# The last batch's order of work is rearranged on three engines, and its tile counts and a weight split move behind it

## The chip, the cores and the metric

The kernel runs on one core of a Trainium2 chip. The metric is the device time of one execution in microseconds, lower is better.

## The reference

Input `x` is 8 batches of 512 tokens, 256 wide. With `xn = layernorm(x)` the output is

```
out = x + attention(xn) + experts(xn)

attention: q, k, v of 16 heads, 16 wide; features elu(q.proj)+1, elu(k.proj)+1 (128 per head)
           kv = sum over tokens of k' v;  attn = q' kv / (q' . sum k');  attn @ W_out.T + b_out
experts:   logits = xn @ Wr + br; the two best of 8 experts, softmax weights over them
           h = gelu(xn @ W1[e] + b1[e]);  sum over e of weight * (h @ W2[e] + b2[e])
```

## The kernel before, in words

Every engine has its own program, and semaphores join them. Matmuls on fp32 data are done as three products of a high and a low part (`mm3`, lines 527 to 529). Banks of PSUM are `F[0..3]`, `WK[0..1]`, `NUM` and `DEN`.

**Attention, batch by batch.** A batch `b` has 32 units `u`. `unit` makes one matmul group into `F[u % 4]`: the k features of a token block for `u < 16` (from the stacked tensor `Sk`), a head's q features for `u >= 16` (from `Sq`). ScalarE's `exp(b, u)` (line 1063) and VectorE's `features(b, u)` (line 1468) turn it into `kp` or `qp`; unit `u` waits until feature `u - 4` is done. Into these 32 units the remaining steps are placed by hand, each engine with its own table of "if u == ...". A batch's attention is finished inside the next batch's units: `attend` (line 623, four groups of heads), ScalarE's `copy_att`, `to_tokens` (632), VectorE's `reciprocals` and `products` (1474, 1480), `to_heads` (640), `at_hi`, `heads_rest` (647), `at_lo`, `project` (24 products), `residual` (1489). The own batch's state is made by four `kv` blocks (605), `copy_kv`, `state_T` (613) and `state`.

`final_iteration(7)` does this for the last batch. TensorE has room there, and `keep_clock` (line 772) puts matmuls without use into it. VectorE also makes the routing tables there: `row_counts`, `blocks_1` to `blocks_5`, `first_tiles_of(1..8)`, `short_blocks` and `tile_table`, a chain of small instructions in which `join()` waits for the one before. `tile_table` raises `route_rdy`.

**Experts.** Tokens were sent to the rows of their experts in DRAM (`xg`) by GpSimd. Then 25 tiles of up to 384 rows run: `ffn1` (eight chunks), gelu, high and low part of h (`hh`, `hl`, line 1740), `ffn2` (three blocks of rows), and GpSimd adds the rows into the output. Tile 0 of expert 0 is mixed with the end of the last batch's attention in a written order on TensorE: `ffn1_last(0)`, `attend(7, 3)`, `ffn1_last(1..3)`, `to_tokens`, `ffn1_last(4..6)`, `to_heads`, `ffn1_last(7)`, `heads_rest`, `ffn2(0,0,0)` for chunks 0 to 5, `project`, and then `ffn2(0,0,0)` for chunks 6 and 7. The last of these needs `hidden_lo(0, 3)`, which stands behind `turn_rows(1)` on VectorE:

```
        hidden_lo(0, 1)
        hidden_lo(0, 2)
        turn_rows(1)
        hidden_lo(0, 3)
```

`turn_rows(1)` (line 1507) waits until tile 1's rows (`gblk`, `gtok`) are loaded.

**Weights and rows.** Expert 0's weights are loaded in two halves, the first when unit 15 is done (semaphore `f_full`), since it takes the memory of `Sk`. GpSimd splits them into high and low parts in four pieces (`split_weights`, lines 1905 and 1907); the second raises `w1_rdy`, the fourth `w_rdy`. SP's queue then runs in this order:

```
        sp.wait_ge(w_rdy, 1)
        load_raw(1)
        sp.wait_ge(route_rdy, 1)
        for e in range(E - 1):
            pad(e + 1)
            other_rows(e)
```

`load_raw(1)` asks for expert 1's 2 MB, `pad` writes zero rows, and `other_rows(0)` loads tile 1's rows once VectorE has freed the last ones (`grow_free`).

Of the kernel before, what the change touches and what calls it, by code (L numbers as in the profile page):

```python
# [25 lines left out]
P = 128  # L26
# [47 lines left out]
def build(nc, x, w_in, proj, w_out, b_out, experts, b1, b2, br, consts, out):  # L74
# [144 lines left out]
    ATT_LAST = [NUM, DEN, WK[0], WK[1]]  # L219
# [304 lines left out]
    def _(pe):  # L524
# [102 lines left out]
        def to_tokens(b, n):  # L627

            if n == 0:
                pe.wait_ge(att_rdy, 4 * b + 4)  # L630
            for c in range(4):
                last = nc.tensor.transpose(TOK_BANK[n][:, c * P:(c + 1) * P], att_sb[:, c, n * P:(n + 1) * P], ident)
            last.then_inc(tok_full, 1)
# [16 lines left out]
        def project(b, i, banks=PROJ_BANK):  # L650

            if i == 0:
                pe.wait_ge(atl_rdy, 2 * b + 2)
            for n in range(2):
# [4 lines left out]
            last.then_inc(proj_full, 1)  # L659
# [115 lines left out]
        def final_iteration(b):  # L775
            for u in range(32):
                unit(b, u)
                if 15 <= u < 22:
                    keep_clock(WK[0])
                if 23 <= u < 28:  # L780
                    keep_clock(DEN)
                if u == 29:
                    pe.wait_ge(att_rdy, 4 * b + 1)
                if u >= 29:
                    keep_clock(NUM)
                if u == 0:
                    pe.wait_ge(o_rdy, 2 * b - 1)
                    attend(b - 1, 2)
                if u == 1:
                    pe.wait_ge(pos_read, b + 1)  # L790
                    attend(b - 1, 3)
                if u == 2:
# [4 lines left out]
                if u == 5:  # L797
                    to_tokens(b - 1, 0)
                    to_tokens(b - 1, 1)
                    to_tokens(b - 1, 2)  # L800
                if u == 7:
                    pe.wait_ge(pos_read, b + 2)
                    to_tokens(b - 1, 3)
                if u == 8:
                    pe.wait_ge(at_rdy, 4 * b - 2)
                    kv(b, 0)
                if u == 10:
                    to_heads(b - 1, 0)
                    to_heads(b - 1, 1)
                if u == 11:  # L810
                    kv(b, 1)
                if u == 12:
                    heads_rest(b - 1, 0)
                    heads_rest(b - 1, 1)
                if u == 14:
                    project(b - 1, 0)
                    project(b - 1, 1)
                if u == 15:
                    kv(b, 2)
                if u == 19:  # L820
                    kv(b, 3)
                if u == 22:
                    pe.wait_ge(kv_rdy, b + 1)
                    state_T(b)
                if u == 24:
                    pe.wait_ge(state_rdy, b + 1)
                    pe.wait_ge(o_rdy, 2 * b + 2)
                    attend(b, 0, ATT_LAST)
                if u == 27:
                    first_rows_T()  # L830
                if u == 28:
                    attend(b, 1, ATT_LAST)
                if u == 31:
                    pe.wait_ge(gxl_rdy, 1)
# [136 lines left out]
        pe.wait_ge(w1_rdy, 1)  # L971
        ffn1_last(0)
# [41 lines left out]
    def _(act):  # L1014
# [136 lines left out]
        def final_iteration(b):  # L1151
            for u in range(32):
                exp(b, u)
                if u == 0:
                    copy_att(b - 1, 1)
                    copy_att(b - 1, 2)
                if u == 1:
                    copy_att(b - 1, 3)
                if u == 9:
                    at_hi(b - 1, 0)  # L1160
                    at_hi(b - 1, 1)
                if u == 11:
                    at_lo(b - 1, 0)
                    at_lo(b - 1, 1)
                if u == 19:
                    copy_kv(b)
                if u == 22:
                    state(b)
                if u == 24:
                    copy_att(b, 0, ATT_LAST)  # L1170
                if u == 28:
                    first_rows_hi()
# [123 lines left out]
    def _(dve):  # L1296
# [173 lines left out]
        def reciprocals(b, n):  # L1470

            dve.wait_ge(tok_full, NT * b + n + 1)
            heads = TOK_BANK[n][:, :].rearrange("p (h c) -> p h c", c=32)
            V.reciprocal(rec[:, n, :], heads[:, :, HD]).then_inc(rec_rdy, 1)

        def products(b, n):

            dve.wait_ge(rec_rdy, NT * b + n + 1)
            heads = TOK_BANK[n][:, :].rearrange("p (h c) -> p h c", c=32)
# [104 lines left out]
        def final_iteration(b):  # L1584
            dve.sem_inc(hl_rdy, 4)
            dve.sem_inc(y_rdy, SUB)
            for u in range(32):
# [3 lines left out]
                if u == 3:  # L1591
                    reciprocals(b - 1, 0)
# [392 lines left out]
```

## Time and profile before

| | us |
|---|---|
| median of 3 runs (lowest to highest) | 700.12 (699.78 to 701.21) |
| the profiled execution's own time | 700.86 |
| its span, first to last instruction | 698.7 |
| TensorE (PE) busy | 682.9 |
| VectorE (DVE) busy | 504.1 |
| ScalarE (ACT) busy | 475.3 |
| GpSimd (POOL) busy | 227.9 |

Times of rows count from the span's start. The last batch runs from about 265 to 298 us, tile 0 from there to 323 us, and the other 24 tiles to the end. The span is 2.16 us shorter than that execution's own time. A matmul's busy time overlaps that of the next; the distance between two starts tells the rate.

### The profile page before, as it was taken

How to read it: one execution, taken by the hardware profiler on the slowest of the kernel's cores; microseconds unless marked ns; L12 is line 12 of the kernel's file. 1: busy time of each engine (PE TensorE's matmuls, PEld its weight loads, DVE VectorE, ACT ScalarE, POOL GpSimd, SP SyncE). 2: the span in 40 equal slices, each digit the busy share in tenths (PEclk: the TensorE clock that was granted, in tenths of full speed). 3: DMA queues.
4: the chain of work that ended last, by engine and by line, in shares of the span. 5: the costliest groups of instructions: out<-in, count | busy, mean ns of one | idle time of the engine just before them, and what ended most of it. 6: DMA issues, size and time to landing. Idle time of an engine off the chain costs nothing.

```text
span 698.7 us, 17362 instructions
## 1 busy us (share of the span) xinstructions
PE 682.9 (98%) x5503; PEld 603.3 (86%) x5504; DVE 504.1 (72%) x1246; ACT 475.3 (68%) x875; POOL 227.9 (33%) x169
## 2 busy tenths in 40 slices
PE   8899999999999998999999999999999999999996
PEld 4666777777777776589999999999999999999996
DVE  8798888888888878748577675556777545577544
ACT  5687969696969696776557775447775444577553
POOL 2053232323232324643232532225233222322422
PEclk9999999999999999999999999999999999999999
DMA  8856474747474647765455663336556333454531
GB/s 266 200 182 170 108 228 106 228 106 228 106 228 106 198 106 223 224 189 142 100 98 118 145 167 46 46 47 106 178 71 167 48 52 53 81 131 107 69 48 23
DMA packets 87205, 91.65 MB, mean 131 GB/s; under 512 B 60049, under 2 KB 73361, under 8 KB 84897
## 3 DMA queue, kind: packets, MB, share of 16 engines
q1 hardware_dynamic: 71426, 59.36, 33.9%
q0 software_dynamic: 13872, 18.75, 15.2%
q10 hardware_dynamic: 1872, 13.11, 5.1%
q8 instruction: 17, 0.28, 0.2%
q14 instruction: 18, 0.15, 0.1%
HBM read 39.32 MB, written 26.67 MB: 94 GB/s over the span
## 4 chain that ended last, share of the span: by engine, by line
PE 82%; DVE 6%; issue 4%; ACT 2%; POOL 2%; DMA 2%; SPq 1%; POOLq 0%; DVEq 0%
PE F L527 9%; PE F L528 9%; PE F L529 9%; PE WK L527 5%; PE F L596 5%; PE WK L529 4%; PE WK L528 4%; PE NUM L527 4%; PE NUM L529 4%; PE NUM L528 4%; PE DEN L605 4%; PE DEN L527 4%; PE DEN L529 4%; PE DEN L528 4%; PE F L590 3%
## 5 line engine op out<-in xcount | busy, mean ns | idle before, releaser
L1932 POOL DMA_INDIRECT out<-ysb,icur x75 | 121.0, 1613 | 270.6 <-DVE ysb L1763 241.0
L1218 ACT ACTIVATE h<-F,b1c 128x384 f32<-128x384 f32 x200 | 112.2, 575 | 140.0 <-PE F L529 131.2
L1740 DVE TENSOR_TENSOR hl<-h,hh 128x768 fp32r<-128x768 f32 x100 | 96.1, 962 | 111.6 <-ACT hh L1222 111.6
L1063 ACT ACTIVATE e_ring<-F 128x512 f32<-128x512 f32 x256 | 145.7, 621 | 38.5 <-PE F L590 35.0
L527 PE MATMUL F<-gxh,wh 128*128 128x384 f32 (+1 forms) x400 | 128.6, 321 | 0.4 <-DVE wl L1641 0.4
L528 PE MATMUL F<-gxl,wh 128*128 128x384 f32 (+1 forms) x400 | 128.0, 320 | 0.0
L529 PE MATMUL F<-gxh,wl 128*128 128x384 f32 (+1 forms) x400 | 128.0, 320 | 0.0
L1866 POOL DMA_INDIRECT xg<-rows,slots x64 | 63.2, 988 | 174.0 <-PE F L590 158.8
L1468 DVE SCALAR_TENSOR_TENSOR kp<-F,e_ring 128x512 f32<-128x512 f32 x128 | 82.7, 680 | 13.2 <-PE DEN L605 6.2
L1468 DVE SCALAR_TENSOR_TENSOR qp<-F,e_ring 128x512 f32<-128x512 f32 x128 | 85.2, 683 | 8.5 <-ACT e_ring L1063 7.0
L1222 ACT ACTIVATE hh<-h 128x768 fp32r<-128x768 f32 x100 | 84.6, 846 | 3.3
L527 PEld LDWEIGHTS F<-gxh,wh 128*128 128x128 f32 x400 | 75.6, 189 | 2.5 <-issue 2.5
L528 PEld LDWEIGHTS F<-gxl,wh 128*128 128x128 f32 x400 | 75.6, 189 | 0.0
L529 PEld LDWEIGHTS F<-gxh,wl 128*128 128x128 f32 x400 | 75.6, 189 | 0.0
L590 PEld LDWEIGHTS F<-stacked_proj,Sk 97*128 97x128 f32 x256 | 38.0, 192 | 26.0 <-issue 13.9
L527 PE MATMUL DEN<-wh,hh 128*128 128x256 f32 x200 | 56.7, 283 | 0.6 <-issue 0.6
L527 PE MATMUL NUM<-wh,hh 128*128 128x256 f32 x200 | 56.6, 283 | 0.2 <-DVE hl L1740 0.2
L528 PE MATMUL DEN<-wl,hh 128*128 128x256 f32 x200 | 56.6, 283 | 0.0
L529 PE MATMUL DEN<-wh,hl 128*128 128x256 f32 x200 | 56.6, 283 | 0.0
L529 PE MATMUL NUM<-wh,hl 128*128 128x256 f32 x200 | 56.5, 283 | 0.0
L528 PE MATMUL NUM<-wl,hh 128*128 128x256 f32 x200 | 56.5, 282 | 0.0
L596 PE MATMUL F<-Sq,stacked_proj 97*128 97x512 f32 x128 | 52.3, 450 | 0.3 <-DVE qp L1468 0.3
(261 smaller groups left out, 1552.6 us busy)
## 6 DMA issues: line engine op xcount, KB each, us to landing
wraw<-experts ACTq DMA_DIRECT2D x12, 1024.0 KB, 6.2
gblk<-xg SPq DMA_DIRECT2D x100, 96.0 KB
Sk<-kdh SPq DMA_DIRECT2D x64, 128.0 KB, 2.3
Sq<-qdh SPq DMA_DIRECT2D x64, 128.0 KB
xin<-x SPq DMA_DIRECT2D x8, 512.0 KB, 5.5
Sk<-kdl SPq DMA_DIRECT2D x32, 128.0 KB, 2.4
Sq<-qdl SPq DMA_DIRECT2D x32, 128.0 KB
xres<-x SPq DMA_DIRECT2D x8, 512.0 KB
```

Of the source, the lines that this page charges most:

```text
L527: nc.tensor.matmul(dst, wh_, mh_, start=first, stop=False)
L528: nc.tensor.matmul(dst, wh_, ml_, start=False, stop=False)
L529: return nc.tensor.matmul(dst, wl_, mh_, start=False, stop=last)
L590: last = nc.tensor.matmul(F[u % 4][:, s * D:(s + 1) * D], Sk[0:SROWS, place_of(pr), n * P:(n + 1) * P], stacked_proj[0:SROWS, 2 * pr:2 * p ...
L596: last = nc.tensor.matmul(F[h % 4][:, :], stacked_proj[0:SROWS, h, :], Sq[0:SROWS, place_of(h // 2), :], start=True, stop=True)
L1063: A(e_ring[:, u % 4, :], F[u % 4][:, :], ACT.Exp, bias=EXP_BIAS, scale=1.0 / DOWN).then_inc(exp_done, 1)
L1218: A(h32[:, m, :], F[m % 4][:, 0:T], ACT.Gelu, bias=b1c[:, w, m:m + 1]).then_inc(gelu, 1)
L1222: A(hh[:, 2 * q:2 * q + 2, :], h32[:, 2 * q:2 * q + 2, :], ACT.Copy).then_inc(hh_rdy, 1)
L1468: V.scalar_tensor_tensor(dst, F[u % 4][:, :], DOWN, e_ring[:, u % 4, :], ALU.max, ALU.min).then_inc(feat, 1)
L1740: V.tensor_tensor(hl[:, 2 * q:2 * q + 2, :], h32[:, 2 * q:2 * q + 2, :], f32(hh[:, 2 * q:2 * q + 2, :]), ALU.subtract).then_inc(hl_rdy, 1)
L1866: pool.indirect_dma_start(xg, bass.IndirectOffsetOnAxis(slots[:, k:k + 1], 0), rows[:, n, :], None, bounds_check=last_row, oob_is_err=Fals ...
L1932: pool.indirect_dma_start(out, bass.IndirectOffsetOnAxis(icur[:, s, :], 0), ysb[:, s, :], None, bounds_check=last_token, compute_op=ALU.ad ...
```

## The change

On all three engines `final_iteration` gets another table. On TensorE `attend(6, 2)` and `attend(6, 3)` stand behind units 2 and 3 (before: 0 and 1), the tokens of batch 6 behind unit 6, its heads behind unit 12. `project(6)` moves from behind unit 14 into four pieces behind units 19 to 22; `state_T` from unit 22 to 20, and the last batch's first attention group from 24 to 22. `keep_clock` goes from fifteen places to six. The tokens' and attention's banks change (`TOK_LAST`, `ATT_LAST`). The wait for `gxl_rdy` moves from `attend(7, 2)` to `ffn1_last(0)`.

On VectorE the routing steps from `blocks_3` on move behind the last feature, as `tile_counts()`; the eight single additions of `first_tiles_of` become three over eight columns. `first_rows_tokens` moves ahead of them, and `hidden_lo(0, 0)` behind the last batch's products. On GpSimd the third split gets a wait for `route_rdy`.

The diff, with unchanged lines cut, and without the two places that give `to_tokens`, `reciprocals` and `products` a parameter for their banks:

```diff
@@ -216,7 +216,8 @@
     PROJ_BANK = [WK[1], NUM]
-    ATT_LAST = [NUM, DEN, WK[0], WK[1]]
+    ATT_LAST = [DEN, NUM, DEN, WK[1]]
+    TOK_LAST = [WK[1], NUM, WK[0], WK[1]]
     PROJ_LAST = [WK[1], WK[0]]
...
@@ -647,16 +648,17 @@
-        def project(b, i, banks=PROJ_BANK):
-
-            if i == 0:
+        def project(b, i, banks=PROJ_BANK, blocks=range(2)):
+
+            if i == 0 and blocks[0] == 0:
                 pe.wait_ge(atl_rdy, 2 * b + 2)
-            for n in range(2):
+            for n in blocks:
                 tok = slice((2 * i + n) * P, (2 * i + n + 1) * P)
...
                                WOh[:, g, :], WOl[:, g, :], g == 0, g == 1)
-            last.then_inc(proj_full, 1)
+            if blocks[-1] == 1:
+                last.then_inc(proj_full, 1)
...
@@ -775,63 +777,67 @@
                 unit(b, u)
-                if 15 <= u < 22:
-                    keep_clock(WK[0])
-                if 23 <= u < 28:
-                    keep_clock(DEN)
-                if u == 29:
-                    pe.wait_ge(att_rdy, 4 * b + 1)
-                if u >= 29:
-                    keep_clock(NUM)
-                if u == 0:
+                if u == 2:
                     pe.wait_ge(o_rdy, 2 * b - 1)
                     attend(b - 1, 2)
-                if u == 1:
-                    pe.wait_ge(pos_read, b + 1)
-                    attend(b - 1, 3)
-                if u == 2:
+                if u == 3:
                     pe.wait_ge(o_rdy, 2 * b)
...
                                      start=True, stop=True).then_inc(pos_full, 1)
-                if u == 5:
-                    to_tokens(b - 1, 0)
-                    to_tokens(b - 1, 1)
-                    to_tokens(b - 1, 2)
+                    pe.wait_ge(pos_read, b + 1)
+                    attend(b - 1, 3)
+                if u == 6:
+                    to_tokens(b - 1, 0, TOK_LAST)
+                    pe.wait_ge(pos_read, b + 2)
+                    to_tokens(b - 1, 1, TOK_LAST)
+                    to_tokens(b - 1, 2, TOK_LAST)
                 if u == 7:
-                    pe.wait_ge(pos_read, b + 2)
-                    to_tokens(b - 1, 3)
+                    kv(b, 0)
                 if u == 8:
-                    pe.wait_ge(at_rdy, 4 * b - 2)
-                    kv(b, 0)
+                    pe.wait_ge(at_rdy, 4 * b - 3)
+                    to_tokens(b - 1, 3, TOK_LAST)
                 if u == 10:
+                    pe.wait_ge(feat, 32 * b + 8)
+                    kv(b, 1)
+                if u == 12:
                     to_heads(b - 1, 0)
                     to_heads(b - 1, 1)
-                if u == 11:
-                    kv(b, 1)
-                if u == 12:
+                if u == 15:
+                    kv(b, 2)
                     heads_rest(b - 1, 0)
                     heads_rest(b - 1, 1)
-                if u == 14:
-                    project(b - 1, 0)
-                    project(b - 1, 1)
-                if u == 15:
-                    kv(b, 2)
+                if u == 16:
+                    keep_clock(NUM)
+                if u in (24, 25):
+                    keep_clock(WK[0])
+                if u == 18:
+                    pe.wait_ge(feat, 32 * b + 16)
+                    kv(b, 3)
                 if u == 19:
-                    kv(b, 3)
-                if u == 22:
+                    project(b - 1, 0, blocks=(0,))
+                if u == 20:
+                    project(b - 1, 0, blocks=(1,))
                     pe.wait_ge(kv_rdy, b + 1)
                     state_T(b)
-                if u == 24:
+                if u == 21:
+                    project(b - 1, 1, blocks=(0,))
+                if u == 22:
+                    project(b - 1, 1, blocks=(1,))
                     pe.wait_ge(state_rdy, b + 1)
+                    pe.wait_ge(feat, 32 * b + 20)
+                    attend(b, 0, ATT_LAST)
+                if u == 26:
+                    pe.wait_ge(o_rdy, 2 * b + 1)
+                    first_rows_T()
+                if u == 27:
                     pe.wait_ge(o_rdy, 2 * b + 2)
-                    attend(b, 0, ATT_LAST)
-                if u == 27:
-                    first_rows_T()
-                if u == 28:
                     attend(b, 1, ATT_LAST)
+                if u == 29:
+                    pe.wait_ge(att_rdy, 4 * b + 1)
+                if u >= 29:
+                    keep_clock(DEN)
                 if u == 31:
-                    pe.wait_ge(gxl_rdy, 1)
                     attend(b, 2, ATT_LAST)
...
@@ -969,6 +975,7 @@
         pe.wait_ge(w1_rdy, 1)
+        pe.wait_ge(gxl_rdy, 1)
         ffn1_last(0)
...
@@ -1153,23 +1160,25 @@
                     copy_att(b - 1, 1)
+                if u == 2:
                     copy_att(b - 1, 2)
-                if u == 1:
+                if u == 3:
                     copy_att(b - 1, 3)
-                if u == 9:
+                if u == 13:
                     at_hi(b - 1, 0)
                     at_hi(b - 1, 1)
-                if u == 11:
+                if u == 16:
                     at_lo(b - 1, 0)
                     at_lo(b - 1, 1)
-                if u == 19:
+                if u == 18:
                     copy_kv(b)
-                if u == 22:
+                if u == 20:
                     state(b)
-                if u == 24:
+                if u == 23:
                     copy_att(b, 0, ATT_LAST)
+                if u == 27:
+                    first_rows_hi()
                 if u == 28:
-                    first_rows_hi()
                     copy_att(b, 1, ATT_LAST)
...
@@ -1588,49 +1597,45 @@
                     dve.sem_inc(grow_free, 1)
-                if u == 3:
-                    reciprocals(b - 1, 0)
-                    reciprocals(b - 1, 1)
-                    products(b - 1, 0)
+                if u == 4:
                     row_counts()
-                if u == 4:
-                    products(b - 1, 1)
-                    reciprocals(b - 1, 2)
+                if u == 6:
+                    reciprocals(b - 1, 0, TOK_LAST)
+                    reciprocals(b - 1, 1, TOK_LAST)
+                    products(b - 1, 0, TOK_LAST)
+                if u == 7:
+                    products(b - 1, 1, TOK_LAST)
+                    reciprocals(b - 1, 2, TOK_LAST)
+                if u == 8:
+                    products(b - 1, 2, TOK_LAST)
+                if u == 9:
+                    reciprocals(b - 1, 3, TOK_LAST)
+                if u == 10:
+                    products(b - 1, 3, TOK_LAST)
+                if u == 12:
                     blocks_1()
-                if u == 5:
-                    products(b - 1, 2)
-                    blocks_2()
-                if u == 6:
-                    reciprocals(b - 1, 3)
-                    blocks_3()
-                    products(b - 1, 3)
-                if u == 8:
-                    blocks_4()
-                if u == 8:
-                    blocks_5()
-                if u == 9:
-                    first_tiles_of(1)
-                    first_tiles_of(2)
-                if u == 10:
-                    first_tiles_of(3)
-                    first_tiles_of(4)
-                    first_tiles_of(5)
-                if u == 11:
-                    first_tiles_of(6)
-                    first_tiles_of(7)
-                    first_tiles_of(8)
-                    short_blocks()
-                if u == 17:
-                    tile_table()
+                if u == 13:
                     dve.wait_ge(s_b1, 16)
                     V.tensor_copy(b1c[:, 0, :], b1T[:, 0:MT]).then_inc(b1_rdy, 1)
-                if u == 18:
+                    blocks_2()
+                if u == 22:
                     residual(b - 1, 0)
-                if u == 19:
+                if u == 24:
                     residual(b - 1, 1)
...
                 features(b, u)
+
+        def tile_counts():
+
+            blocks_3()
+            blocks_4()
+            blocks_5()
+            sums_1()
+            sums_2()
+            sums_4()
+            short_blocks()
+            tile_table()
...
@@ -1642,7 +1647,8 @@
-        cnt, tiles_, first_ = counts[:, 0, 0:E], counts[:, 1, 0:E], counts[:, 2, :]
+        cnt, tiles_, first_ = counts[:, 0, 0:E], counts[:, 1, 4:4 + E], counts[:, 2, :]
+        pairs_, fours_ = counts[:, 6, 4:4 + E], counts[:, 1, 4:4 + E]
         full_, blocks_, limit_ = counts[:, 3, 0:E], counts[:, 4, 0:E], counts[:, 5, 0:E]
...
@@ -1678,12 +1684,19 @@
-        def first_tiles_of(e):
+        def sums_1():
             join()
-            if e == 1:
-                V.scalar_tensor_tensor(full_, tiles_, -2.0, blocks_, ALU.mult, ALU.add)
-            link(V.tensor_tensor(first_[:, e:e + 1], first_[:, e - 1:e], tiles_[:, e - 1:e], ALU.add))
+            V.scalar_tensor_tensor(full_, tiles_, -2.0, blocks_, ALU.mult, ALU.add)
+            link(V.tensor_tensor(pairs_, tiles_, counts[:, 1, 3:3 + E], ALU.add))
+
+        def sums_2():
+            join()
+            link(V.tensor_tensor(fours_, pairs_, counts[:, 6, 2:2 + E], ALU.add))
+
+        def sums_4():
+            join()
+            link(V.tensor_tensor(first_[:, 1:E + 1], fours_, counts[:, 1, 0:E], ALU.add))
...
@@ -1733,6 +1746,9 @@
         final_iteration(NB - 1)
+        dve.wait_ge(grow_ld, FIRST_ROWS_INC)
+        first_rows_tokens()
+        tile_counts()
...
@@ -1784,12 +1800,10 @@
-        hidden_lo(0, 0)
-        dve.wait_ge(grow_ld, FIRST_ROWS_INC)
-        first_rows_tokens()
         for n in range(NT):
...
             products(NB - 1, n)
+        hidden_lo(0, 0)
         hidden_lo(0, 1)
...
@@ -1901,6 +1915,7 @@
                 pool.wait_ge(raw_ld, 16)
+                pool.wait_ge(route_rdy, 1)
             cols = slice(c * PIECE, (c + 1) * PIECE)
```

## Rows read from the trace of the kernel before

**Rows 1.** The page: its first line's engines, and the chain that ended last.

```profile
PE 682.9 (98%) x5503; PEld 603.3 (86%) x5504; DVE 504.1 (72%) x1246; ACT 475.3 (68%) x875; POOL 227.9 (33%) x169
...
PE 82%; DVE 6%; issue 4%; ACT 2%; POOL 2%; DMA 2%; SPq 1%; POOLq 0%; DVEq 0%
```

**Rows 2.** Windows, experts' part: engines' busy us (x count), clock, DMA share, GB/s.

```profile
400.00:500.00 100.00, 100.00 (x750) 100.00 (x749) 63.00 (x129) 60.53 (x97) 28.91 (x19) 1.00 0.45 83
```

**Rows 3.** Chain of waits, last batch and tile 0: start us, us, what.

```profile
265.25 0.99 PE WK L623 x8
...
276.34 1.01 PE DEN L605 x32
...
282.59 5.54 DMA wraw<-experts
...
299.96 2.13 POOL wl L1907
...
309.02 4.78 DMA gtok<-xg
313.82 0.98 DVE gx L1507
```

**Rows 4.** Timeline of PE at tile 0's last chunks: start, us, engine, line.

```profile
315.31 0.28 PE L529 MATMUL WK<-WOh,atl 128*128 128x256 f32 x1
315.79 0.36 PE L527 MATMUL NUM<-wh,hh 128*128 128x256 f32 x1 [0.19 <-DVE hl L1740]
```

**Rows 5.** Timeline of SP's queue, loads of the first rows: start, issue us.

```profile
283.05 5.37 SPq L465 DMA_DIRECT2D grow<-xg  x6
288.46 0.51 SPq L467 DMA_DIRECT2D grow<-xg  x1
```

**Rows 6.** Timeline of POOL: weight splits of expert 0 and the bias.

```profile
295.14 1.04 POOL L1905 CAST wh<-wraw 128x1024 fp32r<-128x1024 f32 x1
...
299.70 2.38 POOL L1907 TENSOR_TENSOR wl<-wraw,wh 128x1024 fp32r<-128x1024 f32 x1
302.05 2.40 POOL L1853 TENSOR_TENSOR xres<-xres,bo_bc 128x1024 f32<-128x1024 f32 x1
```

**Rows 7.** Windows around the load of tile 1's rows, columns as in rows 2.

```profile
302.00:306.00 4.00, 4.00 (x31) 3.96 (x30) 2.08 (x6) 3.55 (x6) 2.44 (x2) 1.00 0.72 219
306.00:310.00 4.00, 4.00 (x27) 3.76 (x26) 3.54 (x9) 3.10 (x5) 0.00 (x0) 1.00 0.97 353
310.00:314.00 4.00, 4.00 (x34) 3.92 (x33) 0.18 (x1) 2.88 (x5) 0.00 (x0) 1.00 0.85 165
```

**Rows 8.** Timeline of DVE in the last batch, gap before in brackets.

```profile
265.71 0.15 DVE L1589 TENSOR_TENSOR totb<-cumb,msum 128x8 bf16<-128x8 bf16 x1
...
277.02 0.54 DVE L1686 TENSOR_TENSOR counts<-counts 128x1 f32<-128x1 f32 x3
...
285.51 0.26 DVE L1698 TENSOR_SCALAR short<-short,cst 128x88 f32<-128x88 f32 x1
...
288.44 3.67 DVE L1468 SCALAR_TENSOR_TENSOR qp<-F,e_ring 128x512 f32<-128x512 f32 x6
...
296.47 1.89 DVE L1468 SCALAR_TENSOR_TENSOR qp<-F,e_ring 128x512 f32<-128x512 f32 x3 [0.20 <-ACT e_ring L1063]
303.88 1.38 DVE L1740 TENSOR_TENSOR hl<-h,hh 128x768 fp32r<-128x768 f32 x1 [5.53 <-ACT hh L1222]
```

**Rows 9.** Timeline of ACT: exponentials in a row.

```profile
279.03 1.58 ACT L1063 ACTIVATE e_ring<-F 128x512 f32<-128x512 f32 x3
```

**Rows 10.** All instructions of line 1740: duration ns min/median/max.

```profile
L1740 DVE TENSOR_TENSOR hl<-h,hh x100: 917/958/1375, 303.9 to 686.1; 128x768 fp32r<-128x768 f32 x100
```

**Rows 11.** Windows in the first batch, columns as in rows 2.

```profile
27.00:27.50 0.50, 0.50 (x3) 0.41 (x2) 0.22 (x1) 0.50 (x2) 0.00 (x0) 0.50 0.91 213
...
30.50:31.00 0.50, 0.50 (x6) 0.50 (x6) 0.50 (x2) 0.50 (x2) 0.00 (x0) 1.00 0.98 221
```

**Rows 12.** Timeline of PE in the first batch: idle before in brackets.

```profile
26.10 0.75 PE L590 MATMUL F<-stacked_proj,Sk 97*128 97x256 f32 x4 [1.54 <-ACT qdl L1043]
```

More of the change, by code:

```diff
@@ L625, in attend, with to_tokens @@
             last.then_inc(attn_done, 1)
-        def to_tokens(b, n):
+        def to_tokens(b, n, banks=TOK_BANK):
             if n == 0:
@@ L631, in to_tokens @@
             for c in range(4):
-                last = nc.tensor.transpose(TOK_BANK[n][:, c * P:(c + 1) * P], att_sb[:, c, n * P:(n + 1) * P], ident)
+                last = nc.tensor.transpose(banks[n][:, c * P:(c + 1) * P], att_sb[:, c, n * P:(n + 1) * P], ident)
             last.then_inc(tok_full, 1)
@@ L1468, in features, with reciprocals, products @@
             V.scalar_tensor_tensor(dst, F[u % 4][:, :], DOWN, e_ring[:, u % 4, :], ALU.max, ALU.min).then_inc(feat, 1)
-        def reciprocals(b, n):
+        def reciprocals(b, n, banks=TOK_BANK):
             dve.wait_ge(tok_full, NT * b + n + 1)
-            heads = TOK_BANK[n][:, :].rearrange("p (h c) -> p h c", c=32)
+            heads = banks[n][:, :].rearrange("p (h c) -> p h c", c=32)
             V.reciprocal(rec[:, n, :], heads[:, :, HD]).then_inc(rec_rdy, 1)
-        def products(b, n):
+        def products(b, n, banks=TOK_BANK):
             dve.wait_ge(rec_rdy, NT * b + n + 1)
-            heads = TOK_BANK[n][:, :].rearrange("p (h c) -> p h c", c=32)
+            heads = banks[n][:, :].rearrange("p (h c) -> p h c", c=32)
             V.tensor_tensor(at[:, n, :].rearrange("p (h d) -> p h d", d=HD), heads[:, :, 0:HD],
```

## The prediction

> **What bounds the kernel now.** I read the page first: TensorE is busy for 682.9 of 698.7 us, and PE is 82% of the chain that ended last [rows 1]. The busy time by windows says how the experts' part behaves: from 400 to 500 us TensorE has no gap at all and the granted clock is 1.00 [rows 2]. So in the experts' part the kernel runs at TensorE's own rate, and a delay that TensorE takes into it from the last batch or tile 0 goes one to one into the time. Then I read the chain of waits over the last batch and tile 0 [rows 3]. It does not run through attention at all. From 282.6 us it is: unit 15 (which frees the memory of `Sk`), the load of the first half of expert 0's weights (5.54 us), four splits on GpSimd until 302.1, SP's queue, the landing of `gtok` at 313.8, the turn of these rows on VectorE, `hl`, and only then TensorE's `ffn2` at 315.79. TensorE's own list shows it finished with the projection at 315.31+0.12 and idle for a moment in front of that matmul [rows 4]. So two paths meet at 315.8: TensorE's own work, and a load chain with 0.4 us or less to spare. A shorter last batch alone gives nothing unless the load chain shortens too.
>
> **The load chain, priced from before.** SP asks for 2 MB of expert 1's weights only behind `w_rdy`, then writes the pad rows, then asks for tile 1's rows, all in one queue [rows 3, 5]. `w_rdy` falls at 302.08 (299.70 + 2.38) [rows 6], the rows land at 313.82: 11.7 us. These 11.7 us are mostly transfer: the DMA engines are 0.72 to 0.97 busy from 302 to 310 and move 4 x (219 + 353 + 165) = 2.9 MB in 12 us [rows 7]. From the landing to TensorE's matmul are 1.97 us. The two splits of the second half take 295.14 to 302.08 = 6.94 us [rows 6]. So before: TensorE resumes at w_rdy + 13.7.
>
> **What the change does to it.** The added `pool.wait_ge(route_rdy, 1)` stands in front of the third split, and `route_rdy` is now raised by `tile_table`, behind all of VectorE's last batch. In the profile `tile_table` ended at 286.1, long before it mattered; now the chain is: last feature of VectorE, first rows' tokens, tile counts, 6.94 us of splits, 11.7, 1.97. Queued behind the waiting split on GpSimd is only `add_bias(7)`, 2.40 us, which feeds a residual that is later anyway. Queued behind `w_rdy` on SP are both weight loads, the pad and the rows. I need the end of VectorE's last batch.
>
> **VectorE's last batch.** Before, from `totb` at 265.71 to the last feature at 296.47+1.89 = 298.36 [rows 8]: 32.65 us, in which the six gaps in front of features are 0.95, 0.70, 1.67, 0.98, 0.67 and 0.20, 5.2 us together (rows 8 show the last of the six). What stays: 32 features at 0.60 (six took 3.67) are 19.2; `totb` and the row counts 0.6, four reciprocals 0.8, four products 1.3, two residuals 1.2, biases and block steps 0.2, first rows' low part 1.0. Together 24.3, so not before 290.0.
> To this come gaps. I replayed the new order by hand with rates of the rows: exponentials 0.50 apart on ScalarE, 0.55 from a unit's matmul to its exponential, a unit on TensorE 0.25, an attention group 1.00, a block of kv 1.01, four transposes 0.45, projection 24 products at 0.12 = 2.9, so 0.73 a piece [rows 3, 9]. Features 0 to 3 start at 265.9, 267.0, 267.6 and 268.6 (attention's copies on ScalarE in between; 265.9, 267.6, 269.0, 270.7 before). Feature 10 starts at 275.7, 1.8 us earlier than before. Unit 15, behind 2.9 us of projection before (282.16), is now ahead of it, at 277.5, and feature 15 starts at 280.0 in place of 283.2. Then gaps return: 0.9 at feature 14 (its exponential stands behind two `at_hi`), 0.8 at feature 17 (behind two `at_lo` and the third kv block), 0.3, 0.6 at features 19 to 21 (behind kv's copy and the state), 0.95 at feature 23 (unit 23 behind the last piece of projection and the first attention group), 0.4 at 28. With 0.9 in the first four and the roundings that is 5.3 again: end at 295.3. One more term: SP's seven loads of the first rows took from 283.05 to 288.97 to issue [rows 5]; now they start near 281, behind the last send, and TensorE wants the rows at 288.4 instead of 292.9. I add 0.3. End 295.6, 2.8 us earlier than before.
>
> **Tile counts.** Eight steps in a row, each joined to the one before. A joined step costs 0.18 (three took 0.54) and `tile_table` with its five instructions took from 285.51 to 286.07 [rows 8]. Seven joins at 0.18, the wider or extra instructions 0.4, the table 0.56: 2.2. First rows' tokens 0.2. So `route_rdy` at 298.0. In the old order VectorE was idle from 298.36 to 303.88, and `hidden_lo(0,0)`, which now stands behind the last batch's products, isn't wanted by TensorE before 307; that cover is ample, and on VectorE this edit costs nothing. The shorter sum (three shifted adds for eight single ones) is worth 0.9 us there.
>
> **TensorE.** `attend(7,3)` waits for feature 31: 295.4 where it ran at 298.72, so it arrives 3.3 us earlier at each later step, and would be through with the projection at 312.1. The nine fillers left out of fifteen are 9 x 0.24 us of work in slack. The first split pair is no hindrance: weights asked at 277.8, landed 5.5 later, splits 6.9: 290.3, before TensorE wants them at 293.6. GpSimd then idles 7.7 us at the gate. Had it gone on, `w_rdy` would have been 297.3.
>
> **The sum.** `w_rdy` = 298.0 + 0.1 + 6.94 + 0.2 = 305.2. The 0.2 is for sharing with VectorE: one `hl` took 1.375 where the median is 0.958 [rows 10], while GpSimd's `add_bias` ran [rows 6], and the new order puts `hidden_lo` beside the last split. Landing +11.7, less 0.3 since SP no longer waits for VectorE's tokens between the pad and the rows: 316.6. TensorE resumes at 316.6 + 1.97 = 318.6 instead of 315.8: +2.8.
> That row shows VectorE waiting for GpSimd, by 0.4. The Trainium skill, SBUF — State Buffer, "Who interferes with whom", says that a VectorE instruction with two SBUF inputs contends with a GpSimd one that reads SBUF, and that the later one waits for the whole instruction; so a GpSimd split may lose as well. By the rule two `hl` ahead of it would make 0.96 x 2 = 1.9 in place of my 0.2, and 4.5 in place of 2.8.
> **The clock.** TensorE would idle from 312.1 to 318.6. In the one place where the trace shows an idle stretch in the middle of work, 1.5 us in front of 26.10, the granted clock is 0.50 (1.2 GHz) from 27.0 on, and 1.00 (2.4 GHz) again at 30.5 [rows 11, 12]. Those 3.2 to 3.5 us of work at half speed lose 1.6. Behind 6.5 idle us I expect the same, part of it in the 0.64 us in which TensorE waits for its registers: 1.4, between 0.5 and 2.
> Total +4.2 on the profiled execution's 700.86 = 705.1; that run lies 0.74 above the median of 700.12, so **704.3**.
>
> **Rivals.**
> Same mechanism, longer: splits blocked by VectorE's `hl`, or the first rows land late and VectorE ends at 297: +1 to +2, 705.3 to 706.3. Within the slower case.
> The clock stays up: 702.9. Against it: in rows 11 and 12 it fell behind 1.5 idle us. Also slower.
> No change: VectorE's last batch has half of my gaps, ends at 292.6, `w_rdy` is 302.1 as before, the resumption is 315.5; with the clock's 1.4, part of it saved: 700 to 701.2. Chance 0.12. Against it: the gaps come from ScalarE's order, which the diff sets.
> Faster: the load chain stops being last. It decides at `w_rdy` 298: then rows land at 309.4 and TensorE, 3.3 us ahead, never stops. With the gate that needs `route_rdy` at 291, below the bound 290.0 + 2.4. What could still do it is a quicker transfer: 2.9 MB at the best rate of rows 7, 353 GB/s, is 8.2 us in place of 11.7. With VectorE's end at 293.5 that gives `w_rdy` at 303.1, a landing at 311.3 and a resumption at 313.3: -2.5, so 697.6 if the clock holds and 699 if it falls. Nothing in the rows makes the same 2.9 MB faster.
> Or TensorE's own path ends last after all, and the whole 3.3 counts: 696.8. Against it, rows 3. Both together 0.14.
>
> **Chances and range.** Slower 0.74, same (within 0.2%, about what a measurement of this kernel tells from no change) 0.12, faster 0.14. In the slower case `route_rdy` between 296.5 and 299.5 gives 702 to 706.5 with the clock's bounds. The range reaches down into the no-change case: 699.8 to 706.5; left out are the faster case and a little above.
>
> **What would show it.** In the changed profile: GpSimd idle for 6 to 8 us in front of its third split, released by VectorE's tile table at about 298; `w_rdy` near 305; rows landing near 316.6; TensorE idle for about 6 us in front of `ffn2(0,0,0)`'s last chunks, released by `hl`; granted clock 0.5 for some 3 us around 318. VectorE's last feature near 295.6. The prediction is wrong if the last batch ends before 293, if the landing comes much less than 11 us behind `w_rdy`, or if the clock holds.

## The result, and the profile after

The changed kernel takes 707.98 us (median of 4 runs, 706.19 to 709.02), the kernel before 700.07 (4 runs) beside it: ratio 1.0105, 95% interval 1.0093 to 1.0118. It is slower, as forecast, but by 7.9 us and not by 4.2, and 1.5 us above the top of the range. The profiled execution has an own time of 707.91 and a span of 705.6.

The page's first line of the changed kernel, as in rows 1:

```profile
PE 682.6 (97%) x5494; PEld 604.3 (86%) x5495; DVE 506.5 (72%) x1241; ACT 474.7 (67%) x875; POOL 227.9 (32%) x169
```

TensorE's busy time is as before, in a span 6.9 us longer. So no work was added; the chain shows where TensorE stands idle. The chain of waits of the changed kernel over the last batch and tile 0 (start us, us, what), to be read beside rows 3:

```profile
275.81 7.08 DMA xg<-rows,slots
282.95 0.38 SPq L466
...
286.12 2.82 DMA grow<-xg
289.07 1.51 PE WK L668 x6
...
299.71 1.05 POOL wh L1920
300.83 2.39 POOL wl L1922
...
304.55 2.15 POOL wl L1922
306.72 0.33 SPq L363
...
314.01 4.88 DMA gtok<-xg
318.92 0.98 DVE gx L1516
319.89 0.85 DVE hl L1756
320.88 0.55 PE NUM L528
```

From the third split on (299.71) this is the forecast chain. Ahead of it stands something that rows 3 don't have: the last send of rows (`xg<-rows,slots`), SP's queue behind it, the landing of the first rows (`grow`), and six transposes of them that take 1.51 us. GpSimd's timeline, beside rows 6 (in brackets the idle time before, and its releaser):

```profile
287.69 2.35 POOL L1922 TENSOR_TENSOR wl<-wraw,wh 128x1024 fp32r<-128x1024 f32 x1
299.71 1.04 POOL L1920 CAST wh<-wraw 128x1024 fp32r<-128x1024 f32 x1 [9.66 <-DVE counts_i L1715]
...
304.28 2.41 POOL L1922 TENSOR_TENSOR wl<-wraw,wh 128x1024 fp32r<-128x1024 f32 x1
306.65 3.11 POOL L1867 TENSOR_TENSOR xres<-xres,bo_bc 128x1024 f32<-128x1024 f32 x1
```

GpSimd stands 9.66 us at the gate, released by the end of the tile counts on VectorE. VectorE's timeline, beside rows 8: `totb`, the last features, the first of the tile counts and their last instruction, three `hl` in a row, and the turn of tile 1's rows.

```profile
264.50 0.16 DVE L1598 TENSOR_TENSOR totb<-cumb,msum 128x8 bf16<-128x8 bf16 x1
...
295.30 1.88 DVE L1477 SCALAR_TENSOR_TENSOR qp<-F,e_ring 128x512 f32<-128x512 f32 x3
297.10 0.17 DVE L1510 COPY wnext<-grow 128x24 f32<-128x24 f32 x1
...
297.60 0.24 DVE L1680 TENSOR_TENSOR first_row<-cst,counts 128x88 int32<-128x88 f32 x1
...
299.41 0.17 DVE L1715 CAST counts_i<-counts 128x9 int32<-128x9 f32 x1
...
304.61 6.83 DVE L1756 TENSOR_TENSOR hl<-h,hh 128x768 fp32r<-128x768 f32 x3
318.92 0.98 DVE L1516 STREAM_TRANSPOSE gx<-gblk 128x768 f32<-128x768 f32 x1 [7.47 <-DMA gtok<-xg]
```

And TensorE's timeline: the two places where it waits longest.

```profile
289.07 1.51 PE L668 MATMUL WK<-cst,grow 128*128 128x128 f32 x6 [2.19 <-DMA grow<-xg]
...
310.63 0.39 PE L528 MATMUL NUM<-wh,hh 128*128 128x256 f32 x1 [0.99 <-DVE hl L1756]
...
320.88 0.55 PE L528 MATMUL NUM<-wh,hh 128*128 128x256 f32 x1 [5.53 <-DVE hl L1756]
```

In the profile of before the first batch ran with the granted clock down for some 3 us [rows 11], in that of after it did not, so the two are compared from `totb`, at 265.71 before [rows 8] and 264.50 after:

| from `totb`, us | before | forecast | after |
|---|---|---|---|
| VectorE's last feature ends | 32.65 | 29.9 | 32.68 |
| `route_rdy` (tile table ends) | 20.4 | 32.3 | 35.08 |
| `w_rdy` | 36.4 | 39.5 | 42.2 |
| tile 1's rows landed | 48.1 | 50.9 | 54.4 |
| TensorE resumes | 50.1 | 52.9 | 56.4 |
| tile 1's first matmul | 57.6 | (61.8) | 65.5 |

Before, tile 1's first matmul started at 323.28 and the span ended 375.4 us later; after, at 330.04 and 375.6. So all of the difference arises in this stage: +8.0 from `totb` to tile 1 (forecast +4.2), less the 1.2 us by which this run was ahead at `totb`, makes 6.8 of the 6.9 between the spans.

### The profile page after: what moved, and what is told of

It reads as the page before. It is cut to its first block, busy times and chain, and to the rows that moved or that the text cites. A ratio compares the mean times of both kernels' runs of the same rounds, so it can differ in the third digit from the quotient of the medians.

```text
span 705.6 us, 17342 instructions
## 1 busy us (share of the span) xinstructions
PE 682.6 (97%) x5494; PEld 604.3 (86%) x5495; DVE 506.5 (72%) x1241; ACT 474.7 (67%) x875; POOL 227.9 (32%) x169
## 4 chain that ended last, share of the span: by engine, by line
PE 81%; DVE 7%; issue 4%; ACT 3%; DMA 2%; SPq 2%; POOL 1%; POOLq 0%; DVEq 0%; ACTq 0%
PE F L528 9%; PE F L529 9%; PE F L530 9%; PE WK L528 5%; PE F L597 5%; PE WK L530 4%; PE WK L529 4%; PE NUM L528 4%; PE NUM L530 4%; PE NUM L529 4%; PE DEN L606 4%; PE DEN L528 4%; PE DEN L529 4%; PE DEN L530 4%; DVE kp L1477 3%
## 5 line engine op out<-in xcount | busy, mean ns | idle before, releaser
L1756 DVE TENSOR_TENSOR hl<-h,hh 128x768 fp32r<-128x768 f32 x100 | 99.7, 999 | 106.4 <-ACT hh L1231 106.4
L530 PE MATMUL NUM<-wh,hl 128*128 128x256 f32 x200 | 56.8, 284 | 0.0
L529 PE MATMUL NUM<-wl,hh 128*128 128x256 f32 x200 | 56.8, 284 | 0.0
```

Source lines behind the costliest of these rows:

```text
L529: nc.tensor.matmul(dst, wh_, ml_, start=False, stop=False)
L530: return nc.tensor.matmul(dst, wl_, mh_, start=False, stop=last)
L1756: V.tensor_tensor(hl[:, 2 * q:2 * q + 2, :], h32[:, 2 * q:2 * q + 2, :], f32(hh[:, 2 * q:2 * q + 2, :]), ALU.subtract).then_inc(hl_rdy, 1)
```

## The experiments

Every kernel ran beside the kernel before on its chip; ratios are to that one, with the 95% interval.

**1. Is it the gate?** (e1_no_gate)

```diff
                 pool.wait_ge(raw_ld, 16)
-                pool.wait_ge(route_rdy, 1)
```

> The changed kernel without GpSimd's wait for route_rdy. Theory A (the loss is the gate: VectorE's end, tile counts, two splits, SP's loads and TensorE's stall stand in one line): the third split starts right behind the second, w_rdy falls about 9.7 us earlier than in the changed kernel (near 32.5 us behind totb instead of 42.2), the rows land before TensorE wants hl, the 5.5 us stall and the slow clock behind it go; time 699.5 to 701. Theory B (the new tables themselves slow the last batch, with the 2.2 us wait for the first rows and the clock's fall behind it): 705 or more. Theory C (the gate protects the tile counts from sharing with GpSimd): the counts take more than 4 us instead of 2.5 and the time stays above 702.

Measured: 700.03 us (11 runs), ratio 0.9986 (0.9975 to 0.9997). The gate carries the whole loss: 1.2% or 8.3 us by the two ratios. GpSimd's third split started at 292.79, when its half of the weights had landed, and `w_rdy` came at 299.76 (+35.3 from `totb`; I had expected +32.5). The stall of 5.5 us is gone. Yet the kernel is hardly faster than the one before, and VectorE's timeline says why (the last line shown is the turn of tile 1's rows):

```profile
294.77 1.53 DVE L1511 COPY inext<-grow 128x3 f32<-128x3 f32 x1
...
297.42 2.44 DVE L1680 TENSOR_TENSOR first_row<-cst,counts 128x88 int32<-128x88 f32 x1
299.79 2.35 DVE L1685 CAST counts<-counts_i 128x8 f32<-128x8 int32 x1
...
303.62 0.17 DVE L1715 CAST counts_i<-counts 128x9 int32<-128x9 f32 x1
...
313.18 0.98 DVE L1516 STREAM_TRANSPOSE gx<-gblk 128x768 f32<-128x768 f32 x1 [4.32 <-DMA gtok<-xg]
```

Beside it GpSimd's:

```profile
293.92 2.37 POOL L1921 TENSOR_TENSOR wl<-wraw,wh 128x1024 fp32r<-128x1024 f32 x1
...
297.36 2.40 POOL L1921 TENSOR_TENSOR wl<-wraw,wh 128x1024 fp32r<-128x1024 f32 x1
299.71 2.40 POOL L1867 TENSOR_TENSOR xres<-xres,bo_bc 128x1024 f32<-128x1024 f32 x1
```

`first_row`, 0.24 us in the changed kernel, takes 2.44 and ends at 299.86, where the split ends at 299.76; the cast of 128x8 behind it takes 2.35 and ends at 302.14, where the bias ends at 302.11; the copy of 128x3 ends at 296.30, the split beside it at 296.29. Each of these small instructions of VectorE lasts until the GpSimd instruction beside it ends. Not every one does: the copy of 128x24 ahead of them, at 294.69, took 0.17 us beside a running split, and no run shows why. The Trainium skill, SBUF — State Buffer, "Who interferes with whom", says that VectorE and GpSimd share a pair of ports as an exclusive lock, that a VectorE instruction with two SBUF inputs contends for it with a GpSimd one that reads SBUF, that copies and casts can, and that issue order decides who blocks; for the three ends named here the trace agrees to 0.1 us.

Tokens and tile counts took 9.1 us instead of 2.5. TensorE then waited 2.23 us for attention's products (`at`), which stand behind them on VectorE. And `route_rdy` came at 303.79, 4.0 us behind `w_rdy`, so that SP, which needs both, began the pad only at 303.81. The rows landed at 313.18, and TensorE waited for the `hl` behind them here too:

```profile
315.15 0.35 PE L528 MATMUL NUM<-wh,hh 128*128 128x256 f32 x1 [1.18 <-DVE hl L1756]
```

Tile 1 begins 58.1 us behind `totb`, before 57.6. So the gate has a use that the prediction didn't see: it keeps the splits off the tile counts, on which the rows hang as well. A kernel without the gate and with SP's order of experiment 5 was not run.

**2. What does the clock cost?** (e2_fill)

```diff
             project(NB - 1, i, PROJ_LAST)
+        for _ in range(24):
+            keep_clock(DEN)
         ffn2(0, 0, 0, range(MT - 2, MT))
```

> The changed kernel with 24 useless matmuls (0.22 us each, 5.3 us together) on TensorE behind the projection, in the stall in front of the last chunks of tile 0's second layer. They end just before hl comes. Theory A: the stall's length stays, but the granted clock stays at 1.00 behind it: 1.7 us less than the changed kernel, about 706.3. Rival (the slow clock costs nothing, since those stretches wait for VectorE anyway): 708.0, no difference.

Measured: 704.79 (5 runs), ratio 1.0057 (1.0044 to 1.0070), 3.4 us less than the changed kernel by the ratios. Windows of this kernel (us, busy time of each engine, clock, DMA share, GB/s), with the fillers and behind them:

```profile
312.00:316.00 4.00, 4.00 (x24) 2.30 (x24) 0.00 (x0) 0.00 (x0) 0.00 (x0) 1.00 0.94 198
316.00:320.00 4.00, 3.20 (x17) 1.59 (x15) 3.35 (x6) 2.33 (x4) 0.00 (x0) 1.00 0.00 0
320.00:324.00 4.00, 3.79 (x32) 3.82 (x33) 3.96 (x11) 2.40 (x3) 0.00 (x0) 1.00 0.32 131
```

The same stretches of the changed kernel, where TensorE is idle and then runs at 0.50:

```profile
316.00:318.00 2.00, 0.00 (x0) 0.00 (x0) 0.00 (x0) 0.00 (x0) 0.00 (x0) 1.00 0.90 119
320.00:326.00 6.00, 5.12 (x22) 4.92 (x23) 5.96 (x13) 4.66 (x6) 0.00 (x0) 0.50 0.21 87
326.00:328.00 2.00, 2.00 (x17) 2.00 (x16) 1.51 (x7) 0.00 (x0) 0.26 (x1) 0.88 0.00 0
```

From the resumption to tile 1 are 9.16 us in the changed kernel and 7.49 before: the clock behind the stall costs 1.67. But 3.4 us came back, so about half of it is from elsewhere. In this kernel's profile TensorE waited 1.47 us for the first rows (2.19 in the changed one), the clock held behind that wait, and `route_rdy` came 32.8 us behind `totb`, not 35.1. The edit stands behind that wait. I take it that the wait varies between executions, as it does between the two profiles of the changed kernel (2.19 and 3.13 us, experiment 10); that this is the other half was not shown.

**3. The gate on the old order of work** (e3_old_tables_gate): the kernel before, with only the tile counts (in their shorter form) and the tokens at the end of the last batch, `hidden_lo(0, 0)` behind the products, and the gate; the orders of TensorE and ScalarE stay old.

```diff
         final_iteration(NB - 1)
+        dve.wait_ge(grow_ld, FIRST_ROWS_INC)
+        first_rows_tokens()
+        tile_counts()
...
                 pool.wait_ge(raw_ld, 16)
+                pool.wait_ge(route_rdy, 1)
```

> The kernel before with only the second half of the change: tile counts behind the last feature, in their shorter form, first rows' tokens ahead of them, the gate on the third split; all tables of the last batch otherwise as before. Theory A: VectorE ends at about 32.3 us behind totb, w_rdy 9.7 us behind that, and TensorE stalls for about 5 to 6 us: 706.5 to 708.5. Theory B (the new tables are the loss): 700 to 702.

Measured: 707.45 (4 runs), ratio 1.0091 (1.0077 to 1.0106). With the gate, the old and the new order can't be told apart. `route_rdy` at +34.6, GpSimd and TensorE:

```profile
299.24 1.04 POOL L1908 CAST wh<-wraw 128x1024 fp32r<-128x1024 f32 x1 [5.72 <-DVE counts_i L1703]
```

```profile
320.27 0.55 PE L527 MATMUL NUM<-wh,hh 128*128 128x256 f32 x1 [5.39 <-DVE hl L1744]
```

Its stall is of the same length as that of the changed kernel. The whole loss belongs to "tile counts at the end, and the gate behind them", and as a whole the new order gave nothing back.

**4. Why are the first rows late?** (e4_sends_first) In the changed kernel SP asks for 1 MB of weights at 275.80, in the same moment in which the last send starts; the send took 7.08 us to land, and SP's loads of the first rows, which wait for it, began only at 282.95. SP's timeline of the changed kernel:

```profile
275.80 0.34 SPq L460 DMA_DIRECT2D wraw<-experts  x1
282.95 3.13 SPq L466 DMA_DIRECT2D grow<-xg  x6
```

The experiment puts the weights behind the sends:

```diff
         sp.wait_ge(f_full, 32 * NB - 16)
+        sp.wait_ge(sent, SENT_INC * NB)
         sp.dma_start(wraw[:, 0:2048], experts[0][:, 0:2048]).then_inc(w1_ld, 16)
```

> The changed kernel with SP waiting for the sends of batch 7 before it asks for the first half of expert 0's weights. Theory A2 (the first rows are late because the last send, 7.1 us to landing, shares the DMA engines with 1 MB of weights that is now asked at the same moment): the sends land 3 us or more earlier, TensorE's 2.2 us wait for the first rows and the clock's fall behind it shrink, VectorE ends 2 to 3 us earlier, and through the gate all of it counts: 704.5 to 706. Rival (the sends just take that long, or the pad rows are in front of them): no difference, 707 to 709.

Measured: 705.94 (6 runs), ratio 1.0068 (1.0053 to 1.0083), 2.6 us less than the changed kernel by the ratios. The loads began at 281.87, 16.1 us behind `totb` instead of 18.4. TensorE:

```profile
289.24 0.85 PE L669 MATMUL WK<-cst,grow 128*128 128x128 f32 x6 [1.13 <-DMA grow<-xg]
```

The send starts at 277.06 and SP is free of it at 281.43, after 4.4 us in place of 7.1. TensorE's wait is 1.13 us, the granted clock stays at 1.00 behind it, and `route_rdy` is at +32.5. The stall in front of `ffn2` is as long as it was, 5.6 us.

**5. The rows ahead of expert 1's weights** (e8_gate_rows_first). If the stall is the load chain `w_rdy` → 2 MB → pad → rows, it should go when SP stops tying the rows to the weights; the gate stays.

```diff
-        sp.wait_ge(w_rdy, 1)
-        load_raw(1)
         sp.wait_ge(route_rdy, 1)
-        for e in range(E - 1):
+        pad(1)
+        _, end_0 = tiles_of(0)
+        with sp.If(end_0 > 1):
+            load_rows(1, row_of(0, 1))
+            sp.wait_ge(w_rdy, 1)
+            load_raw(1)
...
+        sp.wait_ge(pad_st, 32)
+        first_rows(1)
+        for e in range(1, E - 1):
```

> The changed kernel, gate kept, but SP asks for tile 1's rows as soon as route_rdy is there, ahead of expert 1's 2 MB, and only these wait for w_rdy. Theory A in its sharper form (the gate costs time only because the rows stand behind w_rdy and 2 MB in SP's queue): rows land by 42 us behind totb instead of 54.4, TensorE's stall of 5.5 us and the slow clock behind it go, the tile counts keep their 2.5 us; 2 to 3 us below the kernel before, ratio 0.996 to 0.997. Rival (w_rdy itself is what TensorE waits for, in ffn2(0,0,0), or expert 1's weights come too late): ratio 1.002 or more.

Measured: 698.58 (8 runs), ratio 0.9969 (0.9951 to 0.9988). SP's and VectorE's timelines of this kernel:

```profile
303.14 1.91 SPq L476 DMA_DIRECT2D gblk<-xg  x4
305.24 0.39 SPq L478 DMA_DIRECT2D gtok<-xg  x1
306.55 0.36 SPq L363 DMA_DIRECT2D wraw<-experts  x1
```

```profile
304.48 6.80 DVE L1768 TENSOR_TENSOR hl<-h,hh 128x768 fp32r<-128x768 f32 x3
311.21 0.97 DVE L1528 STREAM_TRANSPOSE gx<-gblk 128x768 f32<-128x768 f32 x1
```

The rows are asked for 7.9 us earlier than in the changed kernel (311.03), `gx` stands directly behind the `hl`, TensorE's stall of 5.5 us is gone, and with it 8.9 us of time against the changed kernel on the same chip (experiment 10). The gate is still there: it was only dear because rows and weights were one chain. What TensorE waited for in the changed kernel was not the rows themselves but `hidden_lo(0, 3)`, which stands behind `turn_rows(1)` on VectorE; putting it ahead of `turn_rows(1)` is another way out, and was not run.

**6. The same on the kernel before** (e7_before_rows_first): SP's new order alone.

> The kernel before with SP's new order alone. The load chain of before had under 0.4 us to spare and TensorE waited 0.2 to 0.4 us for hl: the time falls by 0.2 to 0.5 us, ratio 0.999 to 1.000. If the chain of waits misleads and the load chain was in fact longer than TensorE's own work in most executions, it falls by 1 us or more.

Measured: 703.97 (12 runs, 698.49 to 706.16), ratio 1.0028 (1.0005 to 1.0051). I had not expected it slower. The times fall into two groups, four of 698.5 to 700.3 and eight of 702.4 to 706.2. The profile is of the slowest. In its chain of waits stand the rows of tile 2:

```profile
323.84 0.51 SPq L475
324.53 10.78 DMA gtok<-xg
...
336.24 0.93 DVE hl L1752
337.21 0.58 PE NUM L539
```

and on ScalarE's queue, in that same microsecond, 2 MB of expert 2's weights are asked for:

```profile
324.42 0.38 ACTq L362 DMA_DIRECT2D wraw<-experts  x1
```

In the profile of before, SP was done asking for those rows at 325.0 and ScalarE asked at 326.26, and they were in time. Here they landed at 335.3, TensorE stood 5.2 us in front of an `hl`, and the clock fell behind it. That this is what parts the two groups was not shown: only one execution has a trace.

**7. Both repairs, gate kept** (e9_gate_rows_sends_first): experiments 4 and 5 together.

> The same with SP also waiting for the sends of batch 7 before it asks for expert 0's first half. By the run with that alone (first rows asked 16.1 instead of 18.4 us behind totb, TensorE's wait for them 1.1 instead of 2.2) another 0.5 to 1 us less than the run with the rows first; rival: no difference, since the last batch isn't what ends last once TensorE has its fillers, or slower because w1_rdy comes 3.5 us later.

Measured: 698.02 (6 runs, 697.35 to 698.73), ratio 0.9961 (0.9947 to 0.9975). `route_rdy` at +33.0, the clock holds in the last batch (the wait for the first rows is 1.64), tile 1 begins 55.2 us behind `totb` instead of 65.5. It beats both kernels, and is the version that I would keep.

**8. What is the new order worth, then?** (e10_old_tables_gate_rows_first): experiment 3 with SP's order of experiment 5.

> The kernel before with tile counts at the end and the gate, and with SP's new order, but with the old tables of the last batch: against the run with the new tables and the rows first (2.1 us below before) it tells what the new tables are worth. If the tables shorten the last batch (theory of the prediction: 2.8 us, held up by the first rows' landing): this run is at before's time or 1 us below, ratio 0.998 to 1.000. If they give nothing and the gain of that run is from the counts' move and SP's order: ratio 0.996 to 0.997.

Measured: 700.20 (11 runs), ratio 0.9990 (0.9981 to 0.9998). With the old order of TensorE and ScalarE the repaired kernel is as fast as before; with the new one it is 1.5 us faster by the ratios (experiment 5), 2.0 with the sends first as well (experiment 7). It was another chip; the interval overlaps that of experiment 5 and lies apart from that of experiment 7. Experiment 3 against experiment 4, on one chip, gives 1.6 us by the ratios, but the sends too differ there. The profiles agree in part: tile 1 begins 56.8 us behind `totb` here, 55.2 in experiment 7, but 57.2 in that of experiment 5, where the clock fell in the last batch. So where the load chain is free, the new order is worth some 1.5 us, about half of the 2.8 forecast, and that is less sure than the rest.

**9. GpSimd's bias out of the way of the `hl`** (e11_bias_later): experiment 7, and `add_bias(7)` waits for seven `hl`.

```diff
             split_weights(c)
+        pool.wait_ge(hl_rdy, 7)
         add_bias(NB - 1)
```

> The run with gate, rows first and sends first, with GpSimd's bias for the last residual behind the third hl of tile 0. There three hl in a row took 6.8 us where they take 2.7 without GpSimd's splits beside them, and TensorE waited 1.0 us for one. If add_bias (3.1 us, the last GpSimd instruction in that stretch) is what holds hl up, TensorE's wait goes and the time falls by 0.5 to 1.0 us, ratio 0.995; if the two splits ahead of it do, nothing changes, 0.996.

Measured: 698.68 (12 runs, but from 695.53 to 708.85), ratio 0.9962 (0.9942 to 0.9982): no better than experiment 7. In its profile the three `hl` take 4.58 us instead of 6.8, and TensorE's wait of 1.0 us for one of them is gone, as expected; the time didn't follow. But in this execution, with the sends first as in experiment 7, TensorE waited 3.09 us for the first rows, the granted clock fell behind it, and `route_rdy` came at +35.4: sends first do not always cure that wait. Ten of the runs lie between 695.5 and 699.3, two at 703.4 and 708.9; why is open.

**10. The changed kernel again** (c1_changed_again), on the chip of experiments 5 to 7.

> The changed kernel once more, as it is, beside the others of this group on the same chip. Ratio to the kernel before 1.009 to 1.012. If the clock's fall behind the 2.2 us wait for the first rows is chance (it was absent where that wait was 1.3 to 1.5 us), tile counts may end about 32.8 us behind totb instead of 35.1, and the time lies at the lower end.

Measured: 707.49 (6 runs), ratio 1.0097 (1.0079 to 1.0115). The loss repeats, and so do its stages: a wait of 3.13 us for the first rows, `route_rdy` at +35.5, 5.50 us of idle in front of `ffn2`.

## Why the prediction was right or wrong

**The mechanism was right.** GpSimd idle at the gate, released by the tile table; a longer load chain; TensorE idle in front of `ffn2`'s last chunks, released by `hl`; the clock at 0.50 behind: all four are in the profile, and experiments 1 and 5 show that the gate and the tie of rows to weights make the loss. Of the rivals, "longer" was the one that came, by its second cause and not by its first: the splits of GpSimd lost nothing (7.11 us from `route_rdy` to `w_rdy`, 7.24 forecast), since the `hl` began at 304.61, behind the start of the last split (304.28), and it was VectorE that waited. But it came larger than priced: on the time of rows 8, where `totb` is 1.2 us later, VectorE ended its batch at 298.4 and not at 297, and `route_rdy` came at 300.8, above the 299.5 from which the top of the range was worked out.

**The step that failed is the sum of VectorE's last batch**, 295.6 and a gain of 2.8 us. Measured from `totb` the last feature ended at 32.68, before at 32.65: a gain of 0. Inside the sum it is the term for the first rows, "I add 0.3". I let SP's loads start near 281, directly behind a send that I took to be quick (before, SP was free 3.7 us behind its start). But the change puts unit 15, and with it the request for 1 MB, in the same moment as the last send, and the send took 7.08 us; the loads began at 282.95, and TensorE, now in need of the rows earlier, waited 2.19 us. Then the part that I had not at all: behind the wait the granted clock fell, in the middle of the last batch, as this window of the changed kernel shows.

```profile
291.00:292.00 1.00, 1.00 (x9) 0.14 (x8) 0.33 (x1) 0.95 (x3) 0.00 (x0) 0.50 0.93 324
```

I had priced a clock fall for the stall that I expected, and none for a stall of 2 us before it, though rows 11 and 12 show one after 1.54 us. What the fall costs can be read from the kernels in which it didn't happen: `route_rdy` came at +32.8 (experiment 2), +32.5 (experiment 4) and +33.0 (experiment 7), and at +35.1 and +35.5 (the changed kernel twice) and +34.9 (experiment 5), where it did. The forecast was +32.3. So the replay was right to 0.2 to 0.7 where the clock held, and the longer wait with the fall behind it is worth 1.9 to 3.0 us between the two groups; no run takes the wait and the fall apart.

**Tile counts and tokens**: 2.4 forecast, 2.48 measured (297.10 to 299.58).

**From `w_rdy` to the landing**: 11.7 less 0.3 forecast, 12.2 measured, 11.7 before. The 0.3 wasn't there: from the pad's first instruction (307.58) to the first `gblk` (311.03) SP took 3.45 us, and as long before, so the tokens had never held it. The other 0.5 no run takes apart.

**What the gate itself cost**: I wrote that without it `w_rdy` would have been 297.3. Experiment 1 has it at +35.3, which is 301.0 on the time of rows 8: the third split also needs the second half of the weights, and waited 2.30 us for it. It changed nothing in the sum, in which the gate came later still.

**Clock behind the long stall**: 1.4 forecast, 1.67 measured. **TensorE's stall**: 6.5 forecast between its own work's end and the resumption, 5.53 measured: its own work ended 50.9 us behind `totb` in place of 46.4, with the wait for the first rows, the clock behind it, and 0.99 us at an `hl` in between.

Together: 2.8 for VectorE's end, 0.8 for the landing less 0.1 gained at the splits, and 0.3 for the clock make 3.8: the 4.2 forecast becomes 8.0 from `totb` to tile 1. Of the other rivals nothing came: the clock did fall, and the rows landed no sooner behind `w_rdy` than before.

## What to carry to other kernels

When a wait is moved in front of work, follow what hangs behind that work in every queue. Here the gate was harmless for GpSimd's splits and TensorE's use of them; it was dear because SP's queue tied the next tile's rows to the splits' end, and untying them turned +1.0% into -0.3% (-0.4% with the sends first as well). And where a change brings a small load on which an engine waits next to a bulk one, price the small one at what it takes beside the bulk, and each wait of TensorE that follows with a clock fall behind it.

## What the runs showed of the hardware that was not expected

- Instructions of VectorE on a few elements can cost as much as a full GpSimd instruction: 128x88 2.44 us instead of 0.24, a cast of 128x8 2.35. The lock works both ways: in the changed kernel three `hl` took 6.83 us (2.7 in experiment 1, where no split or bias ran beside them), and the `add_bias` among them 3.11 us instead of 2.40 [rows 6].
- A send of rows took 7.08 us to land beside 1 MB on another queue, and the 24 columns of `gtok` 10.78 us beside 2 MB asked for in the same microsecond, 4.9 in the changed kernel. Without the 1 MB beside it (experiment 4) the send took 4.4. In experiment 7, with the rows asked for ahead of the weights and the weights behind the sends, none of TensorE's waits there was over 1.64 us, but in experiment 9, with the same order, the one for the first rows was 3.09.
- The granted clock after a wait of TensorE in this stage: it held after 1.13, 1.34, 1.47 and 1.64 us (experiments 4, 1, 2 and 7), and fell after 2.19, 2.24, 3.09 and 3.13 us (the changed kernel, experiment 5, experiment 9, the changed kernel again). In the first batch a wait of 1.5 us was followed by the fall in the profiles of before and of experiment 4, and not in the others, so its length alone doesn't decide. Around the 5.53 us stall the clock was at 0.50 for 6.8 us, until 326.5, which is 5.6 us past the restart; behind the short waits it was at 0.50 for 3.4 us.
